# Two head pairs to a step in a fused attention kernel, with the programs of all engines reordered

## The reference

```
h = ln(x);  x = attn(h, h,   Wq1, Wk1, Wv1, Wo1) + bo1 + x      16 heads of 64
h = ln(x);  x = attn(h, ctx, Wq2, Wk2, Wv2, Wo2) + bo2 + x
h = ln(x);  x = (a * gelu(gate)) @ W2 + b2 + x,   a, gate = split(h @ Wp + bp)
attn: softmax(q k^T / 8) v @ Wo for each head
```

## Time and profile before

| | |
|---|---|
| median of 3 runs | 3203.68 us (3201.36 to 3205.22) |
| the profiled execution: its time, its span | 3205.43 us, 3203.6 us |
| granted TensorE clock, mean | 0.99 |
| busy, us (share of the span) | PE 3112.9 (97%), PEld 2605.1 (81%), DVE 2426.6 (76%), ACT 1885.0 (59%), POOL 1365.8 (43%) |
| stages, by their first and last output sum | self 84.0 to 1321.1, cross 1407.8 to 2617.6 us, feed forward behind it |
| moved by DMA | 625.02 MB, 195 GB/s over the span, 229 and 240 GB/s in the attention stages |

### The profile page before, as it was taken

The page is one execution under the profiler, slowest core; times in us unless marked ns, Lnnn a source line. Parts: engine busy times, 40 slices in busy tenths (PEclk is TensorE's granted clock), DMA queues, the critical chain, the costliest instruction groups (busy, mean ns, idle before and its releaser), DMA issues. The chain is left out here.

```text
span 3203.6 us, 81927 instructions
## 1 busy us (share of the span) xinstructions
PE 3112.9 (97%) x25600; PEld 2605.1 (81%) x25600; DVE 2426.6 (76%) x4811; ACT 1885.0 (59%) x5999; POOL 1365.8 (43%) x1295
## 2 busy tenths in 40 slices
PE   7999999999999999699999999999999969999999
PEld 6888888888888888578888888888888858888888
DVE  7777777777777777588888888888888855565655
ACT  6666666666666666466666666666666643232232
POOL 4444444444444444355555555555555520000100
PEclk9999999999999999799999999999999989999999
DMA  8888888888888887588888888888888860000100
GB/s 245 229 229 229 229 229 229 229 229 229 229 229 229 229 229 221 166 236 241 239 240 241 240 240 242 238 241 240 241 243 240 239 170 22 31 26 30 35 26 20
DMA packets 464425, 625.02 MB, mean 195 GB/s; under 512 B 57728, under 2 KB 397056, under 8 KB 464128
## 3 DMA queue, kind: packets, MB, share of 16 engines
q1 hardware_dynamic: 460256, 624.09, 67.8%
q10 hardware_dynamic: 4128, 0.41, 0.1%
HBM read 330.71 MB, written 293.60 MB: 195 GB/s over the span
## 5 line engine op out<-in xcount | busy, mean ns | idle before, releaser
L381 POOL TENSOR_TENSOR self_probs<-self_probs,self_row_inv 128x512 f32<-128x512 f32 x512 | 535.2, 1045 | 628.1 <-DVE self_row_inv L577 627.2
L381 POOL TENSOR_TENSOR cross_probs<-cross_probs,cross_row_inv 128x512 f32<-128x512 f32 x512 | 535.2, 1045 | 591.0 <-DVE cross_row_inv L577 591.0
L414 ACT ACTIVATE cross_probs<-cross_ps_s,cross_neg_max 128x256 f32<-128x256 f32 x1024 | 473.8, 472 | 66.9 <-DVE cross_neg_max L552 56.9
L414 ACT ACTIVATE self_probs<-self_ps_s,self_neg_max 128x256 f32<-128x256 f32 x1024 | 473.6, 472 | 55.0 <-DVE self_neg_max L552 54.6
L552 DVE TENSOR_REDUCE cross_neg_max<-cross_ps_s 128x2 f32<-128x512 f32 x512 | 325.1, 675 | 0.9 <-PE cross_ps_s L735 0.9
L552 DVE TENSOR_REDUCE self_neg_max<-self_ps_s 128x2 f32<-128x512 f32 x512 | 325.0, 675 | 0.9 <-PE self_ps_s L735 0.8
L571 DVE STREAM_TRANSPOSE cross_blocks<-cross_probs 128x1024 f32<-128x1024 f32 x256 | 316.1, 1235 | 0.0
L571 DVE STREAM_TRANSPOSE self_blocks<-self_probs 128x1024 f32<-128x1024 f32 x256 | 316.0, 1234 | 0.0
L561 DVE TENSOR_TENSOR self_qk_lo<-self_ps_qk,self_qk_hi 128x512 fp32r<-128x512 f32 x256 | 177.1, 692 | 172.6 <-ACT self_qk_hi L475 172.6
L466 ACT ACTIVATE self_o_hi<-self_ps_o 128x256 fp32r<-128x256 f32 x256 | 98.2, 384 | 341.7 <-PE self_ps_o L753 341.6
L466 ACT ACTIVATE cross_o_hi<-cross_ps_o 128x256 fp32r<-128x256 f32 x256 | 98.3, 384 | 327.3 <-PE cross_ps_o L753 327.3
(11 more groups left out here) (166 smaller groups left out, 9817.5 us busy)
## 6 DMA issues: line engine op xcount, KB each, us to landing
self_turns<-self_blocks SPq DMA_DIRECT2D x1024, 128.0 KB, 2.5
self_probs_t<-self_turns SPq DMA_DIRECT2D x256, 512.0 KB, 4.4
cross_turns<-cross_blocks SPq DMA_DIRECT2D x1024, 128.0 KB, 2.6
cross_probs_t<-cross_turns SPq DMA_DIRECT2D x256, 512.0 KB, 4.5
self_xt<-in_x SPq DMA_DIRECT2D x32, 256.0 KB, 3.8
self_xres<-in_x SPq DMA_DIRECT2D x32, 256.0 KB, 4.0
after_self_attention<-yout SPq DMA_DIRECT2D x32, 256.0 KB, 2.6
cross_xt<-after_self_attention SPq DMA_DIRECT2D x32, 256.0 KB, 3.6
```

Source lines behind the costliest of these rows:

```text
L381: pool.tensor_tensor(probs[:, slot % 2, h], probs[:, slot % 2, h], scale, ALU.mult).then_inc(probs_ready, 1)
L414: last = act.activation(probs[:, slot % 2, h, t], scores[:, slot % 2, h, t], ACT.Exp, bias=neg_max[:, slot % 2, i:i + 1], accum_out=row_su ...
```

## The change

A step now handles two pairs, p and p + 1 (p = 0, 2, 4, 6), and the programs of all engines are written anew for it. The lags become `EXPS` 2, `NORMED` 3 (POOL's product, new as a lag of its own), `TURNED` 4, `LOADED` 6, `WEIGHTED` 6, `PROJECTED` 8. The values are projected and copied in four whole quarters, one per step. POOL multiplies once for a pair (128x1024), DVE takes one reciprocal for a pair (128x4), and `o_hi` and `o_lo` are made for two pairs at once (128x512), since the two weighted sums of a step write the two halves of `ps_o`. The tensor in DRAM through which the transposed blocks go has eight slots for four. SP loads two, then stores two; at p = 6 it waits for the store of y before it reads the residual, and POOL's wait for that store goes. PE no longer waits for `y_added` before a sequence's first output product. Matmuls, transfers and their sizes are the same.

```diff
-SCORES, EXPS, TURNED, LOADED, WEIGHTED, PROJECTED = 1, 2, 3, 5, 6, 7
+SCORES, EXPS, NORMED, TURNED, LOADED, WEIGHTED, PROJECTED = 1, 2, 3, 4, 6, 6, 8
-V_PARTS = ((0, (0,)), (0, (1,)), (1, (0, 1)), (2, (0, 1)), (3, (0,)), (3, (1,)))
-V_STEPS = (0, 1, 2, 4, 6, 7)
-TURN_CONTEXT, TURN_H = 3, 5
+TURN_CONTEXT, TURN_H = 2, 4
-    for p in range(PAIRS):
+    for p in range(0, PAIRS, 2):
         step(0, p, FIRST)
...
-        turns = nc.dram_tensor(tag + "turns", [RING, QUADS, QUAD, QUADS, TURN], F32).ap()
+        turns = nc.dram_tensor(tag + "turns", [PAIRS, QUADS, QUAD, QUADS, TURN], F32).ap()
...
 SP:
             def step(b, p, part):
+                for pair in (p, p + 1):
+                    if alive(part, pair, LOADED):
+                        load_turn(b, pair)
+                for pair in (p, p + 1):
+                    if alive(part, pair, TURNED):
+                        store_turn(b, pair)
                 if part in (FIRST, LOOP) and p == 0:
                     load_next(b + 1)
-                if part in (LOOP, LAST) and p == PROJECTED:
+                if part in (LOOP, LAST) and p == 6:
                     store(b - 1)
+                    sp.wait_ge(y_stored, 16 * b)
                     load_residual(b)
...
 POOL:
+            def normalise(b, p):
+                s = PAIRS * b + p - NORMED
+                slot = (p - NORMED) % RING
+                pool.wait_ge(inv_ready, s + 1)
+                scale = row_inv[:, slot].unsqueeze(2).to_broadcast([P, 2 * TT, SEQ])
+                tile = probs[:, slot % 2].rearrange("p h t k -> p (h t) k")
+                pool.tensor_tensor(tile, tile, scale, ALU.mult).then_inc(probs_ready, 1)
             def step(b, p, part):
+                for pair in (p, p + 1):
+                    if alive(part, pair, NORMED):
+                        normalise(b, pair)
+                if part in (FIRST, LOOP) and p == 0:
                     norm_power(b + 1)
                 if part != FIRST and p == 2:
                     residual(b - 1)
+                if part in (FIRST, LOOP) and p == 6:
+                    low_h(b + 1)
+                    if cross:
+                        low_context(b + 1)
...
 ACT:
             def step(b, p, part):
                 g = PAIRS * b + p
                 if alive(part, p, PROJECTED):
+                    high_o(b, p)
+                if part != DRAIN:
+                    high_parts(g, p)
                 if alive(part, p, EXPS):
+                    for h in range(2):
+                        exps(g - EXPS, (p - EXPS) % RING, h)
                 if part != DRAIN:
                     copy_v(b, p)
+                    if part in (FIRST, LOOP) and p == TURN_H:
+                        scale_shift(b + 1)
+                    if part in (FIRST, LOOP) and p == 6:
+                        high_h(b + 1)
+                        if cross:
+                            high_context(b + 1)
+                    high_parts(g + 1, p + 1)
+                if alive(part, p + 1, EXPS):
+                    for h in range(2):
+                        exps(g + 1 - EXPS, (p + 1 - EXPS) % RING, h)
...
 DVE:
             def step(b, p, part):
                 g = PAIRS * b + p
+                if alive(part, p, TURNED):
+                    turn(b, p)
+                if alive(part, p, NORMED):
+                    inverse(b, p)
                 if alive(part, p, PROJECTED):
+                    low_o(b, p)
                 if part != DRAIN:
                     low_parts(g, p)
+                if alive(part, p + 1, TURNED):
+                    turn(b, p + 1)
+                if alive(part, p + 1, NORMED):
+                    inverse(b, p + 1)
+                if part in (FIRST, LOOP) and p == 0:
+                    norm_stats(b + 1)
+                if part in (FIRST, LOOP) and p == 2:
+                    norm_apply(b + 1)
+                if part != FIRST and p == 6:
+                    output(b - 1)
+                if alive(part, p, SCORES):
+                    maxima(g - SCORES, (p - SCORES) % 2, 0)
+                if part != DRAIN:
+                    low_parts(g + 1, p + 1)
+                if part in (FIRST, LOOP) and p == TURN_CONTEXT and cross:
+                    context_copy(b + 1)
+                if alive(part, p, SCORES):
+                    maxima(g - SCORES, (p - SCORES) % 2, 1)
+                if part in (FIRST, LOOP) and p == 6 and cross:
                     low_context(b + 1)
+                if alive(part, p + 1, SCORES):
                     for h in range(2):
+                        maxima(g + 1 - SCORES, (p + 1 - SCORES) % 2, h)
...
 PE:
             def step(b, p, part):
                 if part != DRAIN:
+                    project_qk(b, p)
                     project_v(b, p, part)
+                for pair in (p, p + 1):
+                    if alive(part, pair, PROJECTED):
+                        project_out(b, pair)
+                if part != DRAIN:
+                    project_qk(b, p + 1)
+                if part in (FIRST, LOOP) and p == TURN_CONTEXT and cross:
+                    transpose_context(b + 1)
+                if part in (FIRST, LOOP) and p == TURN_H:
+                    transpose_h(b + 1)
+                for pair in (p, p + 1):
+                    if alive(part, pair, SCORES):
+                        score(b, pair)
+                for pair in (p, p + 1):
+                    if alive(part, pair, WEIGHTED):
+                        weigh(b, pair)
```

More of the change, by code:

```diff
@@ L684, in transpose_context, with project_qk @@
                 pe.wait_ge(ctx_loaded, 32 * (b + 1))
-                if counts(c := len(V_PARTS) * b - 3):
+                if counts(c := PAIRS // 2 * b - 2):
                     pe.wait_ge(v_ready, c)
                 transposes(ct, c_transposed)
+            def project_qk(b, p):
+                pe.wait_ge(h_hi_ready, b + 1)
+                if counts(c := PAIRS * b + p):
+                    pe.wait_ge(qk_ready, c)
+                project_pair(ps_qk[:, 0:SEQ], p, True, "wq", b + 1 if p == 0 else None)
+                if cross:
+                    pe.wait_ge(c_ready, 2 * (b + 1))
+                project_pair(ps_qk[:, SEQ:2 * SEQ], p, not cross, "wk").then_inc(qk_done, 1)
@@ new lines, in score @@
+            def score(b, p):
+                s = PAIRS * b + p - SCORES
+                slot = (p - SCORES) % 2
+                pe.wait_ge(qk_ready, s + 1)
+                if counts(c := 2 * (s - 1)):
+                    pe.wait_ge(exps_done, c)
+                passes = ((qk_hi, qk_hi), (qk_lo, qk_hi), (qk_hi, qk_lo))
+                for i, (q, k) in enumerate(passes):
+                    for t in range(TT):
+                        for h in range(2):
+                            rows = HEAD_ROWS[h]
+                            last = nc.tensor.matmul(scores[:, slot, h, t], q[rows, slot, t * P:(t + 1) * P],
+                                                    k[rows, slot, SEQ:2 * SEQ], start=i == 0 and t == 0,
+                                                    stop=i == len(passes) - 1 and t == TT - 1,
+                                                    skip_group_check=True)
+                last.then_inc(scores_done, 1)
@@ new lines, in weigh @@
+            def weigh(b, p):
+                q = (p - WEIGHTED) % PAIRS
+                seq = b if p >= WEIGHTED else b - 1
+                pe.wait_ge(v_ready, PAIRS // 2 * seq + q // 2 + 1)
+                if counts(c := PAIRS // 2 * b + (p - WEIGHTED) // 2):
+                    pe.wait_ge(o_ready, c)
+                slot = (p - WEIGHTED) % RING
+                pe.wait_ge(turn_loaded[slot], 16 * (PAIRS // RING * b + (p - WEIGHTED) // RING + 1))
+                turned_t = probs_t[:, slot].rearrange("p (i h t k q) -> p h k t i q", h=2, t=TT, k=TT, q=QUAD)
+                half = q % 2
+                for k in range(TT):
+                    for h in range(2):
+                        c = (2 * q + h) * DHEAD
+                        last = nc.tensor.matmul(
+                            ps_o[DHEAD * h:DHEAD * (h + 1), half * SEQ:(half + 1) * SEQ],
+                            v[:, k, c:c + DHEAD], turned_t[:, h, k], start=k == 0 and half == 0,
+                            stop=k == TT - 1 and half == 1, skip_group_check=True)
+                last.then_inc(pv_done, 1)
```

231 lines of the change are left out of this document (62 added, 169 removed).

## The result

The changed kernel takes **3481.8 us** (median of 4 runs, 3480.5 to 3484.3) against 3204.5: a ratio of 1.0868, 95% interval 1.0849 to 1.0887. The forecast was 3081, 3.8% faster; it is 8.7% slower. The profiled execution's span is 3482.5 us, 279 more than before.

A forecast was written before the change was run, and what follows sets the result against it. PE's own instruction spacing was taken as the bound. Self 31 x 2.1 = 66 and cross 31 x (39.3 - 36.5 - 1.0) = 56, together 122 us less, gave 3081 us, range 3062 to 3105; forecast chance 0.60.

The forecast's parts named there:

- Is everything else in time?: Layout of one double step on DVE, ACT, POOL and SP; all covered but two cross overruns, 1.0 us a sequence.
- extras of at most 1.4 (p = 0, 2) ... end by 6.6 ... Covered: DVE's extra work behind its second reciprocal, at most 1.4 us, ends before the next score ends at 6.4 to 6.8.
- SP: two loads, then two stores (each four issues) in a step: SP's queue per step: a pair's weights, loaded in their step of use, have 8 us for a landing of 4.4.
- D: Rival, chance 0.05: DVE and POOL too slow within a step, above 10.0 us (self) or 9.8 (cross); 3303 us at 10.3.
- The ring: DVE and POOL waiting on each other inside a step, 7.8 to 9.2 us; free while within 8.9 to 9.3.
- The changes of shape: Extra PE time where the matmul shape changes between blocks; fewer changes save 2.1 us a sequence.
- the 0.53: PE time saved per two pairs by fewer shape changes and no slow second scores and sums, in us.
- Rival E: PE's extras belong to a block's start, so second score and sum keep 0.24 of 0.53; 3141 us, chance 0.04.
- Rival C: DVE's operations cost full duration (maximum 0.67 us), low o 0.36 late in every cross step; 3126 us, chance 0.15.
- The plain steps: PE's double steps without waits: 9.3 us in self, 8.9 in cross.
- Low o late by 0.5 at p = 0 and 0.5 at p = 4: Two cross overruns, at p = 6 and p = 2, each idle PE 0.5 us; 1.0 a sequence.
- The context copy: DVE's copy at p = 2 in cross, 0.6 us in DVE's tail, moves low o from 2.5 to 3.1.

The follow-up runs named there:

- load_first: Changed kernel with SP's load of the next x (in cross also the two context loads) at the head of step p = 0; 3183.5 us.
- score_weigh_by_turns: no_store_wait with PE's order score, sum, score, sum in place of score, score, sum, sum; 3180.3 us.
- no_store_wait: load_first with cross's context loads back behind the stores, and POOL, not SP, waiting for y's store at p = 6; 3147.0 us.
- apply_before_inverse: context_on_act with norm_stats of p = 0 ahead of DVE's second transpose and norm_apply of p = 2 ahead of its second reciprocal; 3092.3 us.
- context_on_act: no_store_wait with the copy of the transposed context at p = 2 made by ACT, not DVE; 3126.7 us.

## Why the prediction was wrong

**The step that failed** is "Is everything else in time?", at "extras of at most 1.4 (p = 0, 2) ... end by 6.6 ... Covered", together with "SP: two loads, then two stores (each four issues) in a step". The first prices `norm_stats` by its own instructions and never asks when its input lands. The second leaves `load_next` out of SP's step, though the diff shows it there, behind both stores. What it takes to see it was at hand: by the prediction's own times SP's second store waits for the transpose that ends at 5.2 of the step; in the trace of before a store of four issues takes 1.77 us and x lands 3.8 us (median) after its issue. So x is issued at 7 and comes at 11, wanted at 5.3. That is 5.7 us of DVE; the trace of after has 7.6 and 11.5 from the step's first q matmul (714.5), and waits of 6.4 (self) and 5.6 (cross) a sequence. None of the rivals had it: D had DVE late by its own work in all steps, at 3303, and the runs refute D. The ring fits: with the load early, self runs at 38.1.

**What the failure cost.** Self took 4.34 a sequence more than before, cross 5.22. The first distance of a stage is shorter, so from the first sequence's q to the last one's it is 129 and 155 us, 285 together; the spans differ by 279, and the 6 between them are won outside these stretches. Against load_first a self sequence takes 6.25 more: 4.6 in the step of p = 0, where PE stands, and 1.9 in the step of p = 2, which begins at the lower clock (medians).

**What was right.** The changes of shape: 2.1 a sequence forecast, 40.04 less 37.86 = 2.2 measured once all else is in time; q/k behind output at 0.12, no slow second scores, DVE idle 0.7 to 0.8 before its second transpose (0.9 forecast). score_weigh_by_turns brings 0.34 of the 0.53 back by the order alone. Rival E (the extras belong to a block's head) falls with the same rows, and they agree with what the Trainium skill ("TensorEngine Tiling (Array Packing)", Key Properties) says of a change of tiling mode. Rival C falls too: three maxima in a row take 1.88 us, 0.60 from one to the next, and DVE reaches low o when it was laid out to. The rule of the Trainium skill ("VectorE: DVE Perf Modes", The DRAIN you can't avoid) that the prediction set against the row need not differ from it: the same paragraph says that a next operation that is not held starts earlier. The plain steps of self take 9.33 (9.3), those of cross 8.96 (8.9, where the prediction's own terms, 9.31 less four times 0.12, make 8.8). POOL's whole-pair product takes 1.905, under the 2.09 assumed. Turned blocks land in time in the changed kernel: PE waits 8.2 us in all for them.

**What was sized wrongly in cross.** Low o late by 0.5 at p = 0 and 0.5 at p = 4 was 1.0 of the sum; in no_store_wait it is 1.4, 0.5 (p = 2) and 0.9, together 2.8. The context copy was the cause named for p = 4, and moving it gave 20 us. Missed were DVE's instructions that stretch beside POOL's: 0.87 at p = 0, 0.9 at p = 2 (2.28 for the 1.36 of the earlier trace rows), 0.5 at p = 6 (median 0.97 for 0.42). With the load mended and the rest as changed, the kernel is at 3150 and not at 3081, outside the forecast's range too: 31 x 2.1 us more in cross (39.56 for 37.5, no_store_wait) and 31 x 0.15 in self. So the forecast would have missed without the late load as well.

What keeps 1.4 us at p = 0 of cross in the best version no run took away, but its rows show where DVE loses it, in the step of p = 6 of apply_before_inverse:

```profile
1714.72 0.69 DVE L553 TENSOR_REDUCE cross_neg_max<-cross_ps_s 128x2 f32<-128x512 f32 x1 [0.66 <-PE cross_ps_s L724]
1715.55 0.69 DVE L562 TENSOR_TENSOR cross_qk_lo<-cross_ps_qk,cross_qk_hi 128x512 fp32r<-128x512 f32 x1
1716.16 0.68 DVE L553 TENSOR_REDUCE cross_neg_max<-cross_ps_s 128x2 f32<-128x512 f32 x1
1716.87 0.98 DVE L546 TENSOR_TENSOR cross_c_hi<-cross_c_t,cross_c_hi 64x256 fp32r<-64x256 f32 x1
1717.88 1.29 DVE L553 TENSOR_REDUCE cross_neg_max<-cross_ps_s 128x2 f32<-128x512 f32 x2
1719.20 1.25 DVE L572 STREAM_TRANSPOSE cross_blocks<-cross_probs 128x1024 f32<-128x1024 f32 x1
```
```profile
1716.84 0.73 POOL L356 TENSOR_TENSOR cross_c_lo<-cross_c_t,cross_c_hi 128x256 fp32r<-128x256 f32 x1
```

From the second maximum to the third it is 1.72 us in place of 0.60: `low_context`, which takes 0.98 for 0.42 alone and has POOL's subtraction beside it for 0.70. The low part begins 0.83 behind the first maximum in place of 0.70, which is all that ACT's two copies can have cost there, and the transpose 1.32 behind the last two in place of 1.20. That makes 1.12, 0.13 and 0.12. A version without `low_context` on DVE, or with POOL's subtractions elsewhere, wasn't tried.

## What to carry to other kernels

When a program is written anew for another step, list for each instruction the transfer that it consumes, and where in SP's queue that transfer stands behind waits of its own; the price of an instruction is no use where its input isn't there. A load that was two steps ahead and is now in the same step cost 300 us here, and one call moved in SP's program gave it back. And a gain at the bounding engine is paid out only where all the others are in time: the same 0.34 was worth its size in three of self's four double steps and nothing in cross.

## What was not expected of the hardware

DVE's tensor_scalar (128x2, 128x256) and tensor_tensor (64x256) with all operands in SBUF didn't finish while a POOL operation that had begun before them ran: 0.17 became 1.04, 0.42 became 1.51, each ending within some 0.3 us of POOL's. Where DVE's began first it kept its own time, and POOL's took longer: in load_first at 1755.41 the 64x256 operation took 0.42 and POOL's `c_lo` 1.03, for 0.73 elsewhere. The layer norm's statistics kept their 0.4 each beside a product (L514 at 1739.01 in context_on_act, product from 1739.16 to 1741.05). Maxima and low parts, which read PSUM, kept their 0.69 beside the same products (low part at 707.63 in after, product from 707.21 to 709.11). Before, the 128x2 operation took 0.17 in all 32 places of each stage: the old order has it begin some 0.15 us before a product's end. But two normalise-apply took 1.36 start to start, beside a product of 1.13 us from 1903.83, against 0.62 here where no product runs. The price that I took from before had such a wait in it, and I read it as the operation's own.

The other is that 4.6 us of PE idle were followed by 4 us of matmuls at the lower clock (0.50 in the window from 726 to 730); the earlier trace rows had 1.00 throughout, and the prediction priced PE's stalls by their length alone.
